# Feed-forward product ahead of the q and k projection, and a bf16 part made by GpSimd

## The reference

```python
qkv = x @ attn_w.T + attn_b                       # 16 heads of 8 features
scores = k . q / sqrt(8)                          # masked to key <= query
probs = softmax(scores over the keys)
x = layernorm(x + (probs . v) @ out_w.T + out_b)
scale = max(abs(x), per token) / 127              # the same per column of rhs
acc = round(x / scale) @ round(rhs / rhs_scale)   # int8 values, exact sums
x = layernorm(x + acc * scale * rhs_scale)
```

## Time and profile before

| what | value |
|---|---|
| runs | 243.31 us median of 3 (243.09 to 243.79) |
| profiled execution | 243.84 us, span 242.1 us |
| TensorE busy | 201.0 us, 83% of the span |
| VectorE busy | 189.1 us, 78% |
| ScalarE busy | 159.8 us, 66% |
| GpSimd busy | 136.4 us, 56% |
| mean granted TensorE clock | 0.92 of full speed |

### The profile page before, as it was taken

One profiled execution on the slowest core, in us unless ns is written; L12 is line 12 of the kernel. 1 busy time (PEld: TensorE's weight loads), 2 busy tenths in 40 slices (PEclk: granted clock), 3 DMA queues, 4 the chain that ended last, 5 costly groups with the idle time before them and its releaser, 6 DMA issues.

```text
span 242.1 us, 10958 instructions
## 1 busy us (share of the span) xinstructions
PE 201.0 (83%) x4335; PEld 132.3 (55%) x4335; DVE 189.1 (78%) x593; ACT 159.8 (66%) x349; POOL 136.4 (56%) x273
## 2 busy tenths in 40 slices
PE   6269869899899999989999999998998889998410
PEld 3147645556565656565656565656565556665200
DVE  2819745889888989898989898989899799835521
ACT  3820055667777878786878787878686778796330
POOL 7634053331718585858585858585854343565754
PEclk9855575999999999999999999999999999999975
DMA  5397476939382849585758583957565611010001
GB/s 150 132 245 152 149 145 190 227 114 231 83 230 59 203 132 206 162 178 155 162 160 175 163 179 118 219 157 164 157 139 160 105 28 26 26 47 27 11 12 43
DMA packets 48259, 32.83 MB, mean 136 GB/s; under 512 B 4688, under 2 KB 48208, under 8 KB 48208
## 3 DMA queue, kind: packets, MB, share of 16 engines
q1 hardware_dynamic: 48064, 31.93, 53.6%
q10 hardware_dynamic: 144, 0.20, 0.3%
HBM read 17.17 MB, written 14.68 MB: 132 GB/s over the span
## 4 chain that ended last, share of the span: by engine, by line
PE 43%; DVE 28%; issue 11%; POOL 4%; DMA 3%; ACT 2%; SPq 1%; POOLq 0%; DVEq 0%; ACTq 0%
PE pv_bank L946 11%; DVE query_max L675 9%; PE act_bank L965 6%; PE dve_bank L879 6%; PE dve_bank L1007 4%; DVE ends_max L675 3%; PE dve_bank L956 3%; DVE ffn L774 3%; PE act_bank L870 2%; PE dve_bank L889 2%; DVE heads L723 2%; PE act_bank L1017 2%; DVE stats L785 2%; DMA k_stat<-image 2%; DVE rden L716 2%
## 5 line engine op out<-in xcount | busy, mean ns | idle before, releaser
L494 ACT ACTIVATE probs<-act_bank 128x512 f32<-128x512 f32 x160 | 88.4, 595 | 31.6 <-PE act_bank L889 31.2
L675 DVE TENSOR_REDUCE query_max<-dve_bank 128x2 f32<-128x512 f32 (+1 forms) x96 | 62.9, 681 | 10.1 <-PE dve_bank L889 9.9
L879 PE MATMUL dve_bank<-k_stat,q_move 48*64 48x256 bf16 (+3 forms) x1024 | 63.7, 245 | 5.6 <-DVE query_max L675 2.7
L870 PE MATMUL act_bank<-q_move,k_stat 50*64 50x256 bf16 (+3 forms) x1024 | 60.2, 236 | 0.9 <-issue 0.9
L879 PEld LDWEIGHTS dve_bank<-k_stat,q_move 48*64 48x64 bf16 x1024 | 41.7, 112 | 24.7 <-DVE ends_max L675 6.7
L946 PE MATMUL pv_bank<-probs,v_stat 128*32 128x256 f32 (+3 forms) x1024 | 49.4, 307 | 0.7 <-issue 0.4
L675 DVE TENSOR_REDUCE ends_max<-dve_bank 128x8 f32<-128x512 f32 x64 | 42.9, 679 | 3.6 <-PE dve_bank L889 3.5
L889 PE MATMUL dve_bank<-causal_t,identb 64*64 64x256 bf16 (+1 forms) x320 | 43.5, 263 | 0.2 <-issue 0.2
L889 PE MATMUL act_bank<-causal,identb 64*64 64x256 bf16 (+1 forms) x320 | 41.6, 253 | 0.0
L870 PEld LDWEIGHTS act_bank<-q_move,k_stat 50*64 50x64 bf16 x1024 | 39.3, 108 | 2.1 <-issue 1.4
L446 POOL TENSOR_SCALAR rstd<-moments 128x2 f32<-128x2 f32 x32 | 7.5, 234 | 53.8 <-DVE moments L790 37.4
(11 more groups left out here) (91 smaller groups left out, 339.1 us busy)
## 6 DMA issues: line engine op xcount, KB each, us to landing
image<-qk_parts SPq DMA_DIRECT2D x32, 384.0 KB, 3.3
q_move<-image SPq DMA_DIRECT2D x32, 192.0 KB, 4.3
k_stat<-image SPq DMA_DIRECT2D x32, 192.0 KB, 4.3
xt_in<-xt_dram SPq DMA_DIRECT2D x16, 128.0 KB, 4.6
x_in<-x_dram SPq DMA_DIRECT2D x16, 128.0 KB, 2.2
out_dram<-o SPq DMA_DIRECT2D x16, 128.0 KB, 1.9
q_move<-shift SPq DMA_DIRECT2D x64, 4.0 KB
wqkv<-wqkv_dram ACTq DMA_DIRECT2D x1, 192.0 KB, 2.7
```

The lines of the kernel that those rows point to most:

```text
L494: act.activation(probs[u][:, :], act_bank[at % ACT_BANKS][:, :], ACT.Exp, scale=SCALE).then_inc(act_emptied, 1)
L675: dve.tensor_reduce(top, keys, op=ALU.max, axis=AX.X).then_inc(dve_emptied, 1)
L870: pe.matmul(bank[64 * half:64 * half + 64, at:at + TOK - blk * KB], k_stat[slot][rows, head, blk * KB:(blk + 1) * KB], q_move[slot][rows, ...
L879: pe.matmul(bank[64 * half:64 * half + 64, at:at + keys], q_move[slot][rows, head, blk * KB:keys], k_stat[slot][rows, head, 0:keys], start ...
```

## The change

TensorE makes the feed-forward product of batch b-3 before it projects q and k of batch b+4, no longer after the probabilities product. From the fifth batch on (b above 3), GpSimd makes the middle bf16 part behind its copy, waiting for its own two steps before; VectorE makes it for the first four batches only (in the phases -2 and -1, and before). The computation is the same.

```diff
@@ -59,6 +59,7 @@
 FIRST_WARM = 4
 QK_RING, XT_RING, RING = 4, 6, 3
 XT_FIRST = 4
+POOL_SECOND = 3
 SCALE = float(HD) ** -0.5
 MASKED = -1e30
 MAGIC = 12582912.0
@@ -423,6 +424,9 @@
                     pool.tensor_tensor(qk_rest[:, :, :], qk_f[:, :, :], first,
                                        ALU.subtract).then_inc(qk_split[1], 1)
                     pool.tensor_copy(first_again[b % 2], first).then_inc(qk_split[1], 1)
+                    if b > POOL_SECOND:
+                        wait(pool, qk_split, b, 2)
+                        pool.tensor_copy(second, qk_rest[:, :, :]).then_inc(qk_split[1], 1)
                 else:
                     wait(pool, qk_split, b, 3)
                     pool.tensor_tensor(third, qk_rest[:, :, :], second,
@@ -817,7 +821,7 @@
                         make_shift(b + 1, 1)
                         second_stats(b - 3, 1)
                         scales(b - 2, 2)
-                        if b > -3:
+                        if -3 < b < 0:
                             second_part(b + 4)
 
 
@@ -1056,11 +1060,11 @@
                         turn_zq(b - 3)
                     if u == 3:
                         turn_maxima(b + 1, 0)
+                        feed_forward(b - 3)
                         if b >= 0:
                             project_qk(b + 4, 0)
                             project_qk(b + 4, 1)
                         pv(b, 0)
-                        feed_forward(b - 3)
                     if u == 6:
                         turn_pv(b - 1)
                         pv(b, 1)
```

## The result

| what | before | after |
|---|---|---|
| runs | 243.28 us, median of 4 (243.09 to 243.79) | 252.12 us, median of 4 (250.97 to 254.54) |
| profiled execution | 243.84 us, span 242.1 us | 252.93 us, span 251.2 us |
| the nine phases with a product and a projection | 108.94 us | 116.69 us |
| TensorE busy | 201.0 us | 201.0 us |
| VectorE busy | 189.1 us | 194.8 us |

The changed kernel is slower: 1.0373 times the time before, with an interval of 1.0289 to 1.0457. VectorE gave a cast away in each phase and is nevertheless busier than before, which is the first thing in the table to stop at.

A forecast was written before the change was run, and what follows sets the result against it. The prediction took the order in which TensorE and VectorE hand work to each other as the bound. Seven phases growing 0.94 and two 0.44 add 7.5 us to the 243.31 median: 250.8 us, range 242.6 to 253.0.

The forecast's parts named there:

- The likeliest case: VectorE's small copy is held by GpSimd's subtraction in the middle phases: slower, 250.8 us; chance 0.55.
- product starts after unit 2 is emptied: TensorE's moved product waits for a PSUM bank until VectorE empties unit 2, then 0.14 us of handover.
- unit 4's maximum, later by: VectorE reduces unit 4 at 99.37 instead of 99.25, 0.12 us later, because its scores come later.
- subtraction ahead of the copy by: GpSimd's subtraction starts earlier and VectorE's small copy later, leaving the copy 0.09 us behind instead of 0.13 ahead.
- price of the hold: VectorE's small copy stands still until GpSimd's subtraction ends, so the next maximum starts 0.93 us later.
- Part one: Product moved forward on TensorE: VectorE's 0.54 us wait for it becomes a wait for unit 4's scores, 0.12 later.
- Part two: Cast moved from VectorE to GpSimd's idle time, 0.61 us there; the phase gains 0.11 us, not 0.33.
- What is late next: VectorE's small copy of the joined maxima falls behind GpSimd's subtraction and is held; 0.94 us later in each phase.
- The sum: Over nine phases with product and projection: 7 x 0.94 + 2 x 0.44 = 7.5 us.
- The copy slips through: Rival: VectorE's small copy wins the port against GpSimd; 242.1 to 244.2 us, likeliest 243.4, no change; chance 0.25.
- The product finds its bank free: Rival: the bank wait does not stop TensorE; 241.0 us, up to 242.5, faster; chance 0.15.
- The bank wait at its dearest: Rival: product to projection costs 0.21 us on TensorE, VectorE's copy free; 244.2 us, slower; chance 0.05.

The follow-up runs named there:

- experiment one: The kernel before with only the feed-forward product moved forward, the cast left on VectorE; 251.65 us, ratio 1.0335.
- experiment six: The changed kernel with the product between projections and probabilities product and VectorE's small copy made as a reduction; 240.06 us, ratio 0.9883.
- experiment three: The changed kernel with VectorE's small copy made as a reduction over an axis of length one; ratio 0.9962.
- four: The changed kernel with GpSimd's short copy put ahead of its subtraction; ratio 1.0093.
- experiment five: The changed kernel with the product between the projections and the probabilities product, the small copy still a copy; ratio 0.9952.

## Why the prediction was right

The likeliest case came about, by the mechanism that was forecast: 252.12 us against 250.8, inside the range. Step by step, for the phase shown:

| step | forecast | measured |
|---|---|---|
| product starts after unit 2 is emptied | 0.14 | 0.14 |
| TensorE idle before it | 0.27 | 0.21 |
| product to projection | 0.12 | 0.13 |
| projection to probabilities product | 1.06 | 1.03 |
| from there to the scores | 0.58 | 0.57 |
| scores to unit 4's maximum | 0.57 | 0.57 |
| unit 4's maximum, later by | 0.12 | 0.09 |
| subtraction ahead of the copy by | 0.09 | 0.07 |
| copy ends after the subtraction | 0.03 | 0.03 |
| price of the hold | 0.93 | 0.96 |
| gain from the cast, unit 4 to unit 9 | 0.11 | 0.09 |
| the phase grows by | 0.94 | 0.99 |

*Part one.* The wait for the product did become a wait for unit 4's scores: 0.64 us at 102.55. Removing a wait of 5.7 us brought nothing, since the scores behind it came 0.09 us later than before. From unit 2 to unit 4 it is 102.55 - 99.42 = 3.13 us, against 99.25 - 96.21 = 3.04.

*Part two.* The cast on GpSimd took 0.61 us and lay in idle time, as forecast. Its gain per phase was 0.06, not 0.11: 0.09 from unit 4 to unit 9, and 0.03 given back from the maximum of unit 9 on, which now waits for its scores. The difference of experiment one to the changed kernel, 13.03 - 12.96 = 0.07, says the same a second time.

*What is late next.* GpSimd's residual sum no longer waits for the scaled product but follows its own queue (101.85 + 0.73 = 102.58, its start 102.53). The subtraction thereby starts 103.89 - 102.55 = 1.34 us after unit 4, where it was 100.78 - 99.25 = 1.53 before, and the copy is at 1.41 in the one, 1.40 in the other. The copy did not move against its own neighbours; the subtraction moved past it. The hold that this makes is 0.96 of the 0.99 us. (The prediction puts today's copy inside the gap between lines 421 and 423; by its own rows it starts 100.70 - 100.65 = 0.05 us before the end of line 421. It still takes 0.17 there, so nothing in the sum hangs on this.)

The Trainium skill (SBUF — State Buffer, section Who interferes with whom) states that the one of the two that issues first holds the shared port pair for its whole instruction. The runs agree, by start times: at 0.07, 0.15 and 0.23 us behind the subtraction the copy is held until its end, and at 0.13 and 0.19 ahead it is free. In the six traces that have the copy, 51 of them are held; they start 0.06 to 0.28 us behind a GpSimd instruction, and each ends 0.03 us behind the end of that instruction. The section also says that a reduction never contends with GpSimd on this chip: the 32 reductions of experiment six, 0.169 to 0.171 us, agree, and so does the one of experiment three that started 0.16 us inside the subtraction.

*The sum* came near, 116.69 - 108.94 = 7.75 us in the nine phases against 7.5, but one part of it for another reason. The forecast took seven phases as growing by 0.94 and the two in which GpSimd waited 0.6 us by 0.44 each, because the hold would be shorter there. Those two grew by 0.44 and 0.50, yet their holds are as long as the others (1.08 and 1.13 us). They had been 12.52 and 12.47 us long before, and the lateness that made them longer than 11.97 does not show in the changed kernel's execution. That this number fits is luck. The six phases of 11.97 grew by 0.99, and a third long one (12.12) by 0.85.

All nine came to 12.96 to 12.98, and the hold itself helps to even them out: a copy that comes later behind the subtraction is held for less time and ends where it would have ended. In experiment one the copy shown was 0.15 behind and held for 1.04, the others were 0.06 to 0.07 behind and held for 1.12 to 1.13, and all nine phases last 13.03 to 13.04. In the three kernels with the hold in every phase (the changed one, one and four) no phase is longer than its neighbours; in five of the six others one to three phases are. TensorE's wait for the bank does not do this: it is there in experiment three too, where three phases are longer. What makes TensorE or VectorE late in a phase was not tried.

The profiled execution lies 1.6 us above what the forecast makes of it (252.93 against 243.84 + 7.5 = 251.3). Of this, 0.25 comes from the nine phases, 0.1 from the tail and 1.2 from the ramp: the first output projection starts at 59.08 instead of 57.87. There TensorE stands still for longer in the middle of a group of scores, with no engine named as releaser. Before, then after:

```profile
48.02 0.19 PE L870 MATMUL act_bank<-q_move,k_stat 50*64 50x64 bf16 x1 [0.88 <-issue]
```

```profile
49.22 0.19 PE L874 MATMUL act_bank<-q_move,k_stat 50*64 50x64 bf16 x1 [1.69 <-issue]
```

This pause is at this place in seven of the nine profiles, between 0.65 us (one and three) and 1.88 us (four). In five it is 0.10 us and in six there is none; these are the two kernels with the product between. Whether it varies by itself or with the program's order was not tried, and I do not count its 0.8 us to the change. The other 0.4 us is there before the pause. Of it 0.25 is there before GpSimd makes its first cast of the new kind (VectorE's cast starts at 33.89 instead of 33.64), and that first cast itself holds the small copy, which then takes 0.44 us instead of 0.17. GpSimd, then VectorE, in the ramp of the changed kernel:

```profile
42.19 0.61 POOL L429 CAST qk_parts<-qk_rest 128x512 bf16<-128x512 f32 x1
```

```profile
42.40 0.44 DVE L690 COPY query_max<-query_max 128x16 f32<-128x16 f32 x1
```

So the new cast is harmless in the nine phases by its place and not by its kind. 7.75 + 1.2 + 0.1 in the tail is the 9.1 us between the two spans.

*The rivals.* "The copy slips through" needed a copy that is free at 0.09 us behind; it was held at 0.07, so the rival fell. Its sizes were right: experiment three is that case, with usual phases 0.04 us longer and no change that can be told. "The product finds its bank free" fell here, since TensorE does wait; experiment five makes it true by another order, and gained 0.22 per phase where the rival had 0.26. "The bank wait at its dearest" asked for more than 0.08 per phase left without the hold; it was 0.04.

Two things stay open: where between 0.06 us behind (held) and 0.07 ahead (the nearest free copy, at 198.88 in experiment one) the hold begins, and what the pauses of TensorE are.

## What to carry to other kernels

When work is moved forward, list not only what waits for it but also what it lets start sooner on the other engines; here GpSimd's subtraction gained 0.19 us on a tiny VectorE copy and passed it, which cost more than everything else in the change. Small copies in SBUF on VectorE whose start lies within some tenths of a microsecond of a long GpSimd instruction are worth looking at in the trace: a duration of the same instruction that varies from 0.17 to 1.1 us is the sign. A form that is not held, here a maximum over one element, removes the dependence on the margin and costs nothing.

## What the runs showed that was not expected

The reduction in place of the copy is as fast as the copy at its best (0.170 against 0.175 us). The prediction used the early hold of the earlier trace rows only as a measure; that the kernel before loses 0.78 us by it, and is faster by this one line, is new.

The order with the copy, in five, also showed that a margin of 0.19 us does not protect: in one late phase in nine the copy took 0.96 us, and the phase 1.2 us more than the others, 0.79 of it by the hold.
